# Carrying scores and weights between two orders of 50,000 edges: one-hot products for all 392 columns, or products for 248 and gathers for 144

## The chip, the cores and the metric

One Trainium2 chip, one of its cores. The metric is the device time of one execution in microseconds (us), and a kernel's time is the median of its runs. TensorE is called PE, VectorE DVE, ScalarE ACT, GpSimd POOL and SyncE SP, as in the profile.

## The reference, cut to what matters

The reference is four graph layers over 100,000 nodes (64 values each) and 50,000 edges. The change touches the second layer alone. There every edge has one score, the scores are turned into weights by a softmax over the edges that share a source node, and the weights scale the rows that are summed by target node:

```
e = leaky_relu(h[src] @ a_src + h[dst] @ a_dst, ALPHA)
seg_max = segment_max(e, src)
exp_e = exp(e - seg_max[src])
denom = segment_sum(exp_e, src)
attention = exp_e / denom[src]
h_prime = segment_sum(attention[:, None] * h[src], dst)
```

The edges are stored in the order of their targets. The softmax needs them in the order of their sources. So one value per edge is carried from the first order to the second before the softmax, and one value per edge is carried back after it.

## The kernel before, in words

The edges are padded to EP = 50176 = 128 x 392. A value per edge is one tile of 128 partitions and EF = 392 columns, and edge number i sits in partition i // 392, column i % 392. The prologue sorts the edges by source and leaves two lists in DRAM: EID says which edge of the first order stands at a place of the second, and RANK says at which place of the second order an edge of the first stands. Each is the inverse of the other.

The program is a row of blocks, each with its own instruction streams for the engines, and every block ends with a barrier of all engines. `weigh_edges` (L1591) runs five of them in a row: `pairs_block` makes the scores `e`; `permute_block` with tag `ps` carries them by RANK to `se`; `softmax_block` makes `sa`; `permute_block` with tag `pb` carries that by EID to `al`; a last block stores `al` to DRAM (L1606). Nothing else runs beside them. `mix_block` follows.

`permute_block` (L1450) works without any gather. SP loads the list of target places into `at` (L1467). DVE turns each place into its partition and its column, as floats (L1475 to L1480: `atf`, `near`, `part`, `col`). Then there is one step for each of the 392 columns c of the source. In it DVE makes two one-hot matrices: `lhs` (128 x 128), which has a one where the counter equals `part[:, c]` (L1485), and `rhs` (128 x 392), which has the value where the counter equals `col[:, c]` (L1486). PE multiplies them (L1495) and adds the product into one PSUM tile `sums` of 392 columns, so after 392 steps each value stands at its place. `lhs` and `rhs` have SL = 4 buffers each, and from the fifth step on DVE waits until PE has finished the step four before. At the end DVE copies `sums` to the output tile (L1489). ACT and POOL have nothing to do in the block.

Gathers and scatters elsewhere in the kernel are indirect DMAs that POOL issues, one for each column of 128 indices: L440 (one word per index, in the prologue, in batches of 8 with four semaphores in turn), L1141 (one word per index, into RANK), L802 and L1326 (rows of up to 66 words).

Of the kernel before, what the change touches and what calls it, by code (L numbers as in the profile page):

```python
# [8 lines left out]
I32 = mybir.dt.int32  # L9
# [3 lines left out]
P = 128  # L13
N, D = 100000, 64
E = 50000
# [3 lines left out]
EP = NCH * CH  # L19
EF = EP // P  # L20
# [137 lines left out]
def chunks_of(k, slots, total=NCH):  # L158

    return len(range(k, total, slots))  # L160
# [1286 lines left out]
NEAR = 12582912.0  # L1447


def permute_block(nc, T, C, tag, index, value, out):  # L1450

    with ExitStack() as ctx:
        m = Mem(nc, ctx, tag)
        SL = 4
        at = m.sb("at", [P, EF], I32)
        atf, near, part, col = (m.sb(x, [P, EF]) for x in "atf near part col".split())
        lhs = [m.sb(f"lhs{k}", [P, P]) for k in range(SL)]
        rhs = [m.sb(f"rhs{k}", [P, EF]) for k in range(SL)]  # L1460
        sums = m.ps("sums", [P, EF])
        s_at, s_ch, s_hot, s_mm = (m.sem(x) for x in "at ch hot mm".split())
        block = ctx.enter_context(nc.Block())

        @block.sync
        def _(sp):
            sp.dma_start(at[:, :], T[index][0:EP].rearrange("(p f) -> p f", f=EF)).then_inc(s_at, 16)  # L1467

        @block.vector
        def _(dve):  # L1470
            v = nc.vector
            ch = Chain(dve, s_ch, 0)
            ch.at(0)
            dve.wait_ge(s_at, 16)
            ch(v.tensor_copy(atf[:, :], at[:, :]))  # L1475

            ch(v.tensor_scalar(near[:, :], atf[:, :], 0.5 * (1 - EF), 1.0 / EF, ALU.add, ALU.mult))
            ch(v.tensor_scalar(near[:, :], near[:, :], NEAR, None, ALU.add))
            ch(v.tensor_scalar(part[:, :], near[:, :], -NEAR, None, ALU.add))
            ch(v.scalar_tensor_tensor(col[:, :], part[:, :], float(-EF), atf[:, :], ALU.mult, ALU.add))  # L1480
            for c in range(EF):
                k = c % SL
                if c >= SL:
                    dve.wait_ge(s_mm, c - SL + 1)
                v.tensor_scalar(lhs[k][:, :], C["count"][:, 0:P], part[:, c:c + 1], None, ALU.is_equal)  # L1485
                v.tensor_scalar(rhs[k][:, :], C["count"][:, :], col[:, c:c + 1], value[:, c:c + 1],  # L1486
                                ALU.is_equal, ALU.mult).then_inc(s_hot, 1)
            dve.wait_ge(s_mm, EF)
            ch(v.tensor_copy(out[:, :], sums[:, :]))  # L1489

        @block.tensor
        def _(pe):
            for c in range(EF):
                pe.wait_ge(s_hot, c + 1)
                nc.tensor.matmul(sums[:, :], lhs[c % SL][:, :], rhs[c % SL][:, :], start=(c == 0), stop=(c == EF - 1)  # L1495
                                 ).then_inc(s_mm, 1)
# [94 lines left out]
def weigh_edges(nc, T, C):  # L1591


    with ExitStack() as ctx:
        m = Mem(nc, ctx, "w")
        e, se, sa, al = (m.sb(x, [P, EF]) for x in "e se sa al".split())
        s_st = m.sem("st")
        pairs_block(nc, T, C, e)
        permute_block(nc, T, C, "ps", "RANK", e, se)
        softmax_block(nc, T, C, se, sa)  # L1600
        permute_block(nc, T, C, "pb", "EID", sa, al)
        with nc.Block() as block:

            @block.sync
            def _(sp):
                sp.dma_start(T["AL"].rearrange("(p f) -> p f", f=EF), al[:, :]).then_inc(s_st, 16)  # L1606
                sp.wait_ge(s_st, 16)
# [592 lines left out]
def program(nc, a, out):  # L2200
    T = {}

    def table(name, shape, dt=F32):
        T[name] = nc.dram_tensor(f"t_{name}", shape, dt, kind="Internal").ap()

    for name in ("SCAT", "POS", "PSRC", "KSRC", "KDST"):
        table(name, [EP], I32)
    for name in ("LAST", "KEEP", "ENDM", "ET"):
        table(name, [EP])
    table("XL", [N, XW])  # L2210
    T["EWP"] = nc.dram_tensor("t_EWP", [9, EP], BF16, kind="Internal").ap()
    table("EA", [18, EP])
    table("XSD", [EP, 2 * D])
    table("SSRC", [SORTED + 2])
    table("EID", [SORTED], I32)
    table("RANK", [SORTED], I32)
    table("AL", [EP])
    table("H1", [EP, P])
    table("HR", [EP, D])
    for name in ("D1", "D2", "D3", "HS", "AG", "X3", "HN3"):  # L2220
        table(name, [EP, D])
    for name in ("REL", "KS", "SL", "TL"):
        table(name, [EP])
    with ExitStack() as ctx:
        m = Mem(nc, ctx, "c")
        C = {name: m.sb(name, shape) for name, shape in (
            ("ident", [P, P]), ("att1r", [P, P]), ("att2r", [P, P]), ("att3r", [P, P]), ("att1b", [P, 8]),
            ("att2b", [P, 2]), ("att3b", [P, 4]), ("ones_row", [1, P]), ("wz1", [P, P]), ("we1", [1, P]),
            ("wl2", [P, P]), ("wr2", [P, P]), ("we2", [1, P]), ("wz3", [P, P]), ("we3", [P, P]), ("b1", [P, 1]),
            ("b2", [D, 1]),  # L2230
            ("b1row", [1, P]), ("brow", [1, P]), ("cstk", [P, D]), ("ones_sq", [P, P]),
            ("lng", [P, D]), ("lnb", [P, D]), ("lrg", [P, D]), ("lrb", [P, D]), ("gamma", [P, D]), ("beta", [P, D]),
            ("bias3", [P, D]), ("bias2", [P, D]), ("wca", [P, D]), ("wra", [P, D]), ("w1", [D, D]),
            ("a1", [D, 2]), ("wflat", [P, 2, 2, D]), ("w1t", [P, D]), ("wb", [P, P]), ("wft", [P, 2, P]),
            ("relp", [P, 2]), ("same", [P, EF]), ("count", [P, EF]), ("c3row", [1, D]), ("c3", [P, D]), ("k1", [P, D]), ("k0", [P, D]), ("bl3", [D, 1]), ("bsum", [P, P]))}
        for name in ("we1p", "we2p"):
            C[name] = m.sb(name, [9, P], BF16)
        C["at"] = m.sb("at", [P, 2, EF], I32)
        prologue_block(nc, a, T, C)
        gat_block(nc, a, T, C, "a", 8, P, False)  # L2240
        positions_block(nc, T)
        gat_block(nc, a, T, C, "b", 2, P, True)
        mlp_block(nc, T, C)
        logit_block(nc, T, C)
        weigh_edges(nc, T, C)
        mix_block(nc, T, C)
        relation_block(nc, T, C)
        gat_block(nc, a, T, C, "g", 4, D, False)
        batch_block(nc, T, C)
        finish_block(nc, a, T, out, C)  # L2250
# [24 lines left out]
```

## Time and profile before

| | before |
|---|---|
| median of 3 runs | 7306.34 us (7302.04 to 7308.86) |
| profiled execution, its own time | 7280.67 us |
| profiled execution, span of its instructions | 7278.9 us |
| mean granted PE clock over the span | 0.721 of full speed |
| block `ps`, from the issue of its load to the start of its last copy | 4004.55 to 4269.81 us |
| block `pb`, from its first matmul to the start of its last copy | 4309.0 to 4569.71 us |

The profile shows one execution. A row of a timeline gives the start, the duration, the engine, the line and the operation with the tiles it writes and reads; in square brackets stand the idle time of the engine before it and what ended that. A row of a table by stretch gives each engine's busy time, the number of instructions, and the clock that PE was granted (1.00 is 2.4 GHz, 0.50 is 1.2 GHz). Busy times of DVE and PE instructions overlap at their ends, so a rate is read from the distance of their starts, not from their durations.

### The profile page before, as it was taken

To read this page: it belongs to the slowest core of one execution; us is meant where nothing else is said; L and a number is where in the kernel's file an instruction comes from. 1 tells how busy PE (TensorE), PEld (TensorE's weight loads), DVE (VectorE), ACT (ScalarE), POOL (GpSimd) and SP (SyncE) were. 2 spreads that over 40 slices of the span, in tenths; PEclk is the share of its full clock that TensorE was granted. 3 is DMA by queue.
4 is the path that set the end of the run, shared out by engine and by line. 5 is a ranking of instruction groups with operands and counts; after the bars stand their busy time and mean duration, and the time that the engine had idled before them with its cause. 6 is when DMAs were issued, how large, how long until landed. Compare 5 with 4: busy or idle time off the path is not lost. (4 is left out here: it accounts for less than half of the span.)

```text
span 7278.9 us, 83566 instructions
## 1 busy us (share of the span) xinstructions
PE 3968.5 (55%) x13024; PEld 2369.0 (33%) x13024; DVE 5486.2 (75%) x16937; ACT 3171.6 (44%) x7568; POOL 4455.4 (61%) x4321
## 2 busy tenths in 40 slices
PE   0002666664665665997000989876886766773000
PEld 0000332322333334886000545672332433331000
DVE  4502898986777777887777999776887888886886
ACT  0001666663333333776444000124554666665555
POOL 2777777775777776775776000007664777774776
PEclk9999677776888887555555989558997676665555
DMA  6001555555333332212998000459884555554554
GB/s 190 4 1 34 99 98 98 100 98 81 87 85 84 86 85 61 49 47 57 121 118 102 2 5 1 136 150 129 155 152 108 116 113 115 113 115 110 169 167 136
DMA packets 905930, 687.04 MB, mean 94 GB/s; under 512 B 595425, under 2 KB 744702, under 8 KB 905180
## 3 DMA queue, kind: packets, MB, share of 16 engines
q1 hardware_dynamic: 517168, 403.39, 20.5%
q0 software_dynamic: 137984, 138.92, 18.9%
q10 hardware_dynamic: 250600, 143.02, 6.5%
q14 instruction: 147, 1.20, 0.1%
q8 instruction: 31, 0.51, 0.0%
HBM read 491.06 MB, written 227.24 MB: 99 GB/s over the span
## 5 line engine op out<-in xcount | busy, mean ns | idle before, releaser
L1793 POOL DMA_INDIRECT f_dg<-t_D,c_at x392 | 379.7, 969 | 1132.5 <-POOLq L179 943.3
L802 POOL DMA_INDIRECT b_xg<-t_H,c_at x784 | 828.4, 1057 | 286.0 <-issue 238.6
L802 POOL DMA_INDIRECT g_xg<-t_D,c_at x784 | 801.7, 1023 | 319.9 <-issue 237.7
L802 POOL DMA_INDIRECT a_xg<-t_XL,c_at x784 | 824.6, 1052 | 250.1 <-issue 238.7
L2181 POOL DMA_INDIRECT out<-n_yo,c_at x392 | 430.8, 1099 | 237.5 <-issue 116.0
L440 POOL DMA_INDIRECT t_XL<-su_pos,su_scatx x392 | 388.2, 990 | 244.7 <-DMA t_XL<-in_nodes 125.7
L1326 POOL DMA_INDIRECT l_d<-t_D,l_ix x392 | 399.3, 1019 | 174.8 <-issue 115.8
L1141 POOL DMA_INDIRECT t_RANK<-m_place,m_at x392 | 400.8, 1022 | 160.9 <-issue 115.7
L938 ACT ACTIVATE a_hn<-a_xg,a_sm 128x64 f32<-128x64 f32 x784 | 269.9, 429 | 399.0 <-DVE a_sm L675 398.0
L1375 ACT ACTIVATE l_hn<-l_xs,l_sm 128x64 f32<-128x64 f32 x784 | 265.0, 426 | 284.0 <-DVE l_sm L675 218.9
L2160 ACT ACTIVATE n_h<-n_x,n_sm 128x64 f32<-128x64 f32 (+1 forms) x800 | 269.4, 426 | 210.0 <-DVE n_sm L675 210.0
L1915 ACT ACTIVATE f_hn<-f_xs,f_bykind 128x64 f32<-128x64 f32 x784 | 265.1, 426 | 178.9 <-DVE f_bykind L1825 178.9
L1032 PE MATMUL b_bank<-c_ident,b_xg 128*128 128x128 f32 x392 | 93.6, 383 | 415.4 <-DMA b_xg<-t_H,c_at 415.4
L1060 PE MATMUL a_bank<-a_zt,c_att1r 128*128 128x512 f32 x196 | 196.4, 1105 | 221.2 <-DVE a_zt L850 221.2
L1416 PE MATMUL pr_prow<-c_ident,pr_col 128*1 128x128 f32 x2 | 0.6, 395 | 567.0 <-DVE pr_col L1434 567.0
L1035 PE MATMUL a_bank<-c_ident,a_hn 128*128 128x128 f32 x392 | 108.4, 432 | 369.1 <-ACT a_hn L938 369.0
L938 ACT ACTIVATE g_hn<-g_xg,g_sm 128x64 f32<-128x64 f32 x784 | 269.6, 427 | 76.4 <-DVE g_sm L675 76.2
L1060 PE MATMUL g_bank<-g_zt,c_att3r 128*128 128x512 f32 x196 | 159.5, 907 | 258.2 <-DVE g_zt L850 258.2
L958 ACT ACTIVATE b_hT<-b_bank 128x512 f32<-128x512 f32 x98 | 58.5, 597 | 521.1 <-PE b_bank L1035 521.1
L1253 ACT ACTIVATE m_xn<-m_pa,m_sm 128x64 f32<-128x64 f32 x784 | 242.4, 414 | 90.5 <-DVE m_sm L675 89.1
L1704 ACT ACTIVATE e_ng<-e_pw 128x256 f32<-128x256 f32 x98 | 37.5, 383 | 535.2 <-PE e_pw L1695 535.2
L1495 PE MATMUL pb_sums<-pb_rhs,pb_lhs 128*128 128x392 f32 x784 | 260.6, 496 | 11.3 <-DVE pb_rhs L1486 11.3
(451 smaller groups left out, 13667.4 us busy)
## 6 DMA issues: line engine op xcount, KB each, us to landing
a_ends<-t_LAST SPq DMA_DIRECT2D x98, 256.0 KB
t_XSD<-a_xg SPq DMA_DIRECT2D x98, 256.0 KB
t_H<-a_oE ACTq DMA_DIRECT2D x98, 256.0 KB
b_ends<-t_LAST SPq DMA_DIRECT2D x98, 256.0 KB
l_xb<-t_XSD SPq DMA_DIRECT2D x49, 512.0 KB
f_rl<-t_REL SPq DMA_DIRECT2D x49, 512.0 KB
g_xb<-t_XSD SPq DMA_DIRECT2D x98, 256.0 KB
g_ends<-t_LAST SPq DMA_DIRECT2D x98, 256.0 KB
```

The costliest lines, as they stand in the source:

```text
L440: nc.gpsimd.indirect_dma_start(lp, bass.IndirectOffsetOnAxis(ap=scatx[:, f:f + 1], axis=0), pos[:, f:f + 1].bitcast(F32), None, bounds_che ...
L802: nc.gpsimd.indirect_dma_start(xg[k][:, j, i, :], None, table, bass.IndirectOffsetOnAxis(ap=C["at"][:, i, n * J + j:n * J + j + 1], axis=0 ...
L938: last = f(hn[k][:, g // 2, g % 2, :], xg[k][:, g // 2, g % 2, 0:D], ACT.Relu, bias=sm[:, 5, g:g + 1], scale=sm[:, 4, g:g + 1])
L1060: mm(bS[:, :], att[:, :], zt[k][:, :], start=True, stop=True).then_inc(S["s"], 1)
L1141: nc.gpsimd.indirect_dma_start(rank, bass.IndirectOffsetOnAxis(ap=at[k][:, j:j + 1], axis=0), place[k][:, j:j + 1], None).then_inc(s_rank[ ...
L1326: nc.gpsimd.indirect_dma_start(d1[k][:, 0, j, :], None, T["D1"], bass.IndirectOffsetOnAxis(ap=ix[k][:, j:j + 1], axis=0)).then_inc(s_g[k], 16)
L1375: last = nc.scalar.activation(hn[k][:, g % 2, g // 2, :], xs[k][:, g // 2, g % 2, :], ACT.Relu, bias=sm[:, 5, g:g + 1], scale=sm[:, 4, g:g ...
L1495: nc.tensor.matmul(sums[:, :], lhs[c % SL][:, :], rhs[c % SL][:, :], start=(c == 0), stop=(c == EF - 1)).then_inc(s_mm, 1)
L1793: nc.gpsimd.indirect_dma_start(dg[k][:, u, j, :], None, T["D2"], bass.IndirectOffsetOnAxis(ap=C["at"][:, 0, (2 * n + u) * J + j:(2 * n + u ...
L1915: last = f(hn[k][:, g // J, g % J, c, :], xs[k][:, g // J, g % J, :], ACT.Relu, bias=by_kind[:, c, 1, g:g + 1], scale=by_kind[:, c, 0, g:g ...
L2160: last = f(h[k][0:np_, g, :], x[k][0:np_, g, :], ACT.Relu, bias=sm[0:np_, 5, g:g + 1], scale=sm[0:np_, 4, g:g + 1])
L2181: nc.gpsimd.indirect_dma_start(out, bass.IndirectOffsetOnAxis(ap=C["at"][:, 0, j:j + 1], axis=0), yo[:, j, :], None, bounds_check=N - 1, o ...
```

## The change: what it does

`permute_block` takes a second list, the inverse of the first, and splits the 392 result columns in two. Columns 0 to 247 are made by products as before: `rhs`, `sums` and the last copy are 248 wide, and there are still 392 steps of `lhs`, `rhs` and product. Columns 248 to 391 are fetched: ACT stores the value tile to a table in DRAM (new tables Vps and Vpb), SP loads the part of the inverse list that belongs to these columns into `of`, DVE clears those columns of the output, and when all three are done POOL issues 144 indirect DMAs. Each fetches 128 single words of the table into one column. They go in 18 batches of 8 with four semaphores in turn, so that a batch waits for the one four before it. POOL ends its part when all have landed. Both calls of `permute_block` get it.

```diff
--- before.py
+++ after.py
@@ -1447,7 +1447,11 @@
 NEAR = 12582912.0
 
 
-def permute_block(nc, T, C, tag, index, value, out):
+BY_GATHER = 144
+BY_PRODUCT = EF - BY_GATHER
+
+
+def permute_block(nc, T, C, tag, index, inverse, value, out):
 
 
 
@@ -1457,20 +1461,45 @@
         at = m.sb("at", [P, EF], I32)
         atf, near, part, col = (m.sb(x, [P, EF]) for x in "atf near part col".split())
         lhs = [m.sb(f"lhs{k}", [P, P]) for k in range(SL)]
-        rhs = [m.sb(f"rhs{k}", [P, EF]) for k in range(SL)]
-        sums = m.ps("sums", [P, EF])
-        s_at, s_ch, s_hot, s_mm = (m.sem(x) for x in "at ch hot mm".split())
+        rhs = [m.sb(f"rhs{k}", [P, BY_PRODUCT]) for k in range(SL)]
+        of = m.sb("of", [P, BY_GATHER], I32)
+        sums = m.ps("sums", [P, BY_PRODUCT])
+        s_at, s_ch, s_hot, s_mm, s_of, s_value, s_clear = (m.sem(x) for x in "at ch hot mm of value clear".split())
+        s_g = m.sems("g", 4)
         block = ctx.enter_context(nc.Block())
+        full = lambda t: t.rearrange("(p f) -> p f", f=EF)
 
         @block.sync
         def _(sp):
-            sp.dma_start(at[:, :], T[index][0:EP].rearrange("(p f) -> p f", f=EF)).then_inc(s_at, 16)
+            sp.dma_start(at[:, :], full(T[index][0:EP])).then_inc(s_at, 16)
+            sp.dma_start(of[:, :], full(T[inverse][0:EP])[:, BY_PRODUCT:EF]).then_inc(s_of, 16)
+
+        @block.scalar
+        def _(act):
+            act.dma_start(full(T["V" + tag]), value[:, :]).then_inc(s_value, 16)
+
+        @block.gpsimd
+        def _(pool):
+            pool.wait_ge(s_of, 16)
+            pool.wait_ge(s_value, 16)
+            pool.wait_ge(s_clear, 1)
+            for b in range(BY_GATHER // 8):
+                k = b % 4
+                if b >= 4:
+                    pool.wait_ge(s_g[k], 16 * 8 * (b // 4))
+                for f in range(8 * b, 8 * b + 8):
+                    nc.gpsimd.indirect_dma_start(out[:, BY_PRODUCT + f:BY_PRODUCT + f + 1], None, T["V" + tag].unsqueeze(1),
+                                                 bass.IndirectOffsetOnAxis(ap=of[:, f:f + 1], axis=0),
+                                                 bounds_check=E - 1, oob_is_err=False).then_inc(s_g[k], 16)
+            for k in range(4):
+                pool.wait_ge(s_g[k], 16 * 8 * chunks_of(k, 4, BY_GATHER // 8))
 
         @block.vector
         def _(dve):
             v = nc.vector
             ch = Chain(dve, s_ch, 0)
             ch.at(0)
+            v.memset(out[:, BY_PRODUCT:EF], 0.0).then_inc(s_clear, 1)
             dve.wait_ge(s_at, 16)
             ch(v.tensor_copy(atf[:, :], at[:, :]))
 
@@ -1483,10 +1512,10 @@
                 if c >= SL:
                     dve.wait_ge(s_mm, c - SL + 1)
                 v.tensor_scalar(lhs[k][:, :], C["count"][:, 0:P], part[:, c:c + 1], None, ALU.is_equal)
-                v.tensor_scalar(rhs[k][:, :], C["count"][:, :], col[:, c:c + 1], value[:, c:c + 1],
+                v.tensor_scalar(rhs[k][:, :], C["count"][:, 0:BY_PRODUCT], col[:, c:c + 1], value[:, c:c + 1],
                                 ALU.is_equal, ALU.mult).then_inc(s_hot, 1)
             dve.wait_ge(s_mm, EF)
-            ch(v.tensor_copy(out[:, :], sums[:, :]))
+            ch(v.tensor_copy(out[:, 0:BY_PRODUCT], sums[:, :]))
 
         @block.tensor
         def _(pe):
@@ -1596,9 +1625,9 @@
         e, se, sa, al = (m.sb(x, [P, EF]) for x in "e se sa al".split())
         s_st = m.sem("st")
         pairs_block(nc, T, C, e)
-        permute_block(nc, T, C, "ps", "RANK", e, se)
+        permute_block(nc, T, C, "ps", "RANK", "EID", e, se)
         softmax_block(nc, T, C, se, sa)
-        permute_block(nc, T, C, "pb", "EID", sa, al)
+        permute_block(nc, T, C, "pb", "EID", "RANK", sa, al)
         with nc.Block() as block:
 
             @block.sync
@@ -2219,7 +2248,7 @@
     table("HR", [EP, D])
     for name in ("D1", "D2", "D3", "HS", "AG", "X3", "HN3"):
         table(name, [EP, D])
-    for name in ("REL", "KS", "SL", "TL"):
+    for name in ("REL", "KS", "SL", "TL", "Vps", "Vpb"):
         table(name, [EP])
     with ExitStack() as ctx:
         m = Mem(nc, ctx, "c")
```

## Rows read from the trace of the kernel before

**Rows 1.** Busy time of each engine over the whole span (page, part 1).

```profile
PE 3968.5 (55%) x13024; PEld 2369.0 (33%) x13024; DVE 5486.2 (75%) x16937; ACT 3171.6 (44%) x7568; POOL 4455.4 (61%) x4321
```

**Rows 2.** Busy us by stretch inside ps and pb; PE, PEld, DVE, ACT, POOL, clock, DMA.

```profile
4050.00:4250.00 200.00, 200.00 (x609) 115.47 (x608) 200.00 (x608) 0.00 (x0) 0.00 (x0) 1.00 0.00 1
4350.00:4550.00 200.00, 200.00 (x609) 115.48 (x608) 200.00 (x609) 0.00 (x0) 0.00 (x0) 1.00 0.00 1
```

**Rows 3.** Timeline, start of block ps: load, first four steps, first wait.

```profile
4004.55 0.33 SPq L1467 DMA_DIRECT2D ps_at<-t_RANK  x1
4006.68 0.36 DVE L1475 CAST ps_atf<-ps_at 128x392 f32<-128x392 int32 x1 [2.84 <-DMA ps_at<-t_RANK]
...
4009.48 0.28 DVE L1485 TENSOR_SCALAR ps_lhs<-c_count,ps_part 128x128 f32<-128x128 f32 x1
...
4009.68 0.48 DVE L1486 TENSOR_SCALAR ps_rhs<-c_count,ps_col,w_e 128x392 f32<-128x392 f32 x1
4010.07 0.28 DVE L1485 TENSOR_SCALAR ps_lhs<-c_count,ps_part 128x128 f32<-128x128 f32 x1
...
4012.64 0.29 DVE L1485 TENSOR_SCALAR ps_lhs<-c_count,ps_part 128x128 f32<-128x128 f32 x1 [0.62 <-PE ps_sums L1495]
```

**Rows 4.** Timeline, end of block ps: the last step's first instruction, the copy.

```profile
4267.18 0.29 DVE L1485 TENSOR_SCALAR ps_lhs<-c_count,ps_part 128x128 f32<-128x128 f32 x1
...
4269.81 0.57 DVE L1489 COPY w_se<-ps_sums 128x392 f32<-128x392 f32 x1 [1.95 <-PE ps_sums L1495]
```

**Rows 5.** Lines L667 and L378, TENSOR_SCALAR of DVE: count, ns min/median/max, starts.

```profile
L667 DVE TENSOR_SCALAR a_sm<-a_sm x98: 171/194/427, 667.9 to 1723.0; 128x8 int32<-128x8 int32 x98
...
L378 DVE TENSOR_SCALAR su_sign<-su_bits x16: 426/428/599, 110.2 to 254.6; 128x512 f32<-128x512 int32 x16
```

**Rows 6.** The store of the last block and the next block's first load.

```profile
4571.17 0.34 SPq L1606 DMA_DIRECT2D t_AL<-w_al  x1
4573.86 0.33 SPq L1642 DMA_DIRECT2D e_hs<-t_HS  x1
```

**Rows 7.** Busy us by stretch, three stages with POOL issuing indirect DMAs (L440, L802, L1141).

```profile
500.00:600.00 100.00, 0.00 (x0) 0.00 (x0) 0.00 (x0) 0.00 (x0) 75.99 (x79) 1.00 0.02 1
1000.00:1200.00 200.00, 135.74 (x351) 61.40 (x352) 179.31 (x551) 123.69 (x291) 155.19 (x148) 0.70 0.54 98
3000.00:3200.00 200.00, 182.71 (x846) 161.27 (x846) 176.67 (x919) 149.35 (x425) 154.27 (x151) 0.50 0.19 48
```

**Rows 8.** Timeline: two instances of L667, each inside one indirect DMA.

```profile
3606.12 0.94 POOL L1326 DMA_INDIRECT l_d<-t_D,l_ix  x1 [0.30 <-issue]
3606.79 0.27 DVE L667 TENSOR_SCALAR l_sm<-l_sm 128x16 int32<-128x16 int32 x1
...
677.13 0.94 POOL L802 DMA_INDIRECT a_xg<-t_XL,c_at  x1 [0.30 <-issue]
...
677.85 0.22 DVE L667 TENSOR_SCALAR a_sm<-a_sm 128x8 int32<-128x8 int32 x1
```

**Rows 9.** Timeline: two large TENSOR_SCALAR back to back beside an indirect DMA.

```profile
203.25 1.16 POOL L440 DMA_INDIRECT t_XL<-su_pos,su_scatx  x1 [0.30 <-issue]
203.60 0.43 DVE L376 TENSOR_SCALAR su_bits<-su_gray 128x512 int32<-128x512 int32 x1
204.06 0.60 DVE L378 TENSOR_SCALAR su_sign<-su_bits 128x512 f32<-128x512 int32 x1
...
204.71 0.97 POOL L440 DMA_INDIRECT t_XL<-su_pos,su_scatx  x1 [0.30 <-issue]
```

**Rows 10.** Timeline: POOL and a long DVE instruction that read SBUF together.

```profile
3602.52 1.23 DVE L1342 TENSOR_TENSOR l_xs<-l_d,l_xb 128x1024 f32<-128x1024 f32 x1 [2.96 <-DMA l_d<-t_D,l_ix]
3602.57 1.99 POOL L1326 DMA_INDIRECT l_d<-t_D,l_ix  x1 [0.30 <-issue]
```

**Rows 11.** Busy us by stretch: stages where PE is less busy than in ps.

```profile
800.00:1000.00 200.00, 134.62 (x348) 59.92 (x348) 180.25 (x546) 127.16 (x301) 155.19 (x148) 0.72 0.54 100
5100.00:5300.00 200.00, 177.89 (x534) 73.20 (x533) 174.89 (x540) 110.63 (x304) 130.54 (x135) 0.93 0.88 155
```

## The prediction

> **What bounds the kernel now.** The page's busy times come first [rows 1]. They name no bound for this change: DVE's 75% is a mean over stages, and `permute_block` runs alone between barriers. So I read its two blocks by stretch [rows 2]. PE and DVE are both busy for all of each 200 us, POOL and ACT do nothing, and PE has its full clock, 2.4 GHz. 609 product instructions, two for a step, make 304.5 steps in 200 us: 0.657 us a step. Which of the two engines sets this shows at the start of the block. In its first steps, with free buffers, DVE starts an `lhs` every 0.59 us (4009.48, 4010.07), 0.20 us of it for `lhs` and 0.39 for `rhs`; after four buffers it waits for PE [rows 3]. PE is the bound, and DVE is only 10% faster. From the first `lhs`, one step of 0.59 us before the 4009.48 [rows 3], to the last at 4267.18 the steps take 258.3 us; then 2.6 us pass to the copy [rows 4]. Seen from the issue of the load at 4004.55, the copy starts after 265.3 us.
>
> **The products.** A product of 248 columns instead of 392 takes 0.657 x 248/392 = 0.416 us of PE. DVE's `lhs` stays at 0.20. For `rhs` I need the price of a column. A one-input instruction took 0.428 us for 512 columns [rows 5] and 0.36 for 392 [rows 3], which is 0.55 ns each. If the whole distance between the 0.20 us slot of 128 columns and the 0.39 us slot of 392 were width, it would be 0.72 ns, the upper end. I take 0.55, which compares instructions without a pointer in both widths: 144 x 0.55 = 0.08 us. DVE's step becomes 0.51 us. So the bound moves from PE (0.416) to DVE (0.51), and only part of PE's 37% arrives: 392 x 0.51 = 200 us. With 0.72 ns it would be 0.486 and 191 us.
>
> **The load, the store, the clear, the copy.** The new store and the second load are issued beside the old load, by ACT and behind it on SP's queue; nothing waits behind them. DVE first used the old load 2.1 us after its issue [rows 3]; for three transfers together I add 1 us, between 0 and 2. The clear of 144 columns goes into DVE's 2.8 us wait for the load [rows 3]; without that cover it is under 0.6 us, the copy of 392 columns [rows 4]. The last copy is narrower (under 0.2 us gained). PE no longer lags by four buffers, so of the 2.6 us before the copy about 1 goes. These cancel.
>
> **The gathers.** POOL needs the store to have landed. A store of the same size and the barrier after it fit into 2.7 us [rows 6], so I start the gathers 3 us after the block's first issue. 144 follow. POOL alone issued 79 in 100 us, 1.27 us each; with DVE 90% busy beside it 148 in 200 us, 1.35 each, and 151 in another stage, 1.32 [rows 7]. With 2 us for the last to land (the load's 2.1) the end is 5 + 144 x 1.35 = 199 us. The traffic is small, 128 words an instruction; the stage at 151 in 200 us moved single words too [rows 7]. So the gathers lie beside the products as long as one costs less than (231 - 5)/144 = 1.57 us, 231 being the end of the products below.
>
> **What they do to each other.** In no stretch of the kernel do wide one-input DVE instructions run without a break beside POOL, so this cost is bounded. A TENSOR_SCALAR that takes 0.171 us took up to 0.427 beside a gather [rows 5]. Two of these late ones end in the same hundredth as the POOL instruction around them (3606.79 + 0.27 = 3606.12 + 0.94; 677.85 + 0.22 = 677.13 + 0.94) [rows 8]. So POOL seems to hold something late in each indirect DMA that DVE needs, for up to 0.256 us. A wide one lost 0.171 us (0.599 against 0.428) [rows 5, 9]. POOL also waits: beside a long two-input instruction its 0.94 became 1.99 [rows 10]. With DVE at work without a gap I take 0.171 us lost per gather, since that row has DVE's shape of instruction: 144 x 0.171 = 25 us on DVE, which now bounds. The ends are 0 and 0.256 + 0.171 = 0.427 (both losses in each gather), 61 us. No gain is possible from a wait. For POOL I allow the 0.19 us that its instruction lost beside that pair (1.16 against 0.97 for the next at that line) [rows 9]: 1.35 + 0.19 = 1.54, ending at 227, still hidden, but barely.
>
> The Trainium skill, "SBUF — State Buffer", section "Who interferes with whom", says more than the row: DVE in a two-port mode and GpSimd exclude each other for the whole of an instruction, whoever starts first. The row shows a hold of at most 0.256 us of 0.94, so here it agrees only in kind. What the whole rule would cost is the third rival.
>
> **The sum.** The step phase becomes 200 + 25 = 225 us instead of 258.3; the copy starts 4.3 + 225 + 1.6 = 231 us after the block's first issue. That is 33 us less, twice 33 = 66 us. On the profiled execution, 7280.7 us (1.8 more than its span), this gives 7215; the median of the runs is 25.6 higher, and against it I predict 7306 - 66 = 7240 us. This case's own range: with no loss and 191 us, 67 less per block, 7172; with the loss at 0.427, 261 us, nothing gained, 7306.
>
> **The rivals.**
> *The gathers end the block but late by less than the gain.* At 1.7 us a gather the end is 5 + 245 = 250 us instead of 265.3: 15 less per block, 7276. For it speaks that my 1.54 is near 1.57. Against it: 1.35 in stages with DVE 90% busy.
> *The gathers starve (slower).* POOL finds DVE in its way at every issue. The point from which it decides is (265.3 - 5)/144 = 1.81 us a gather. At 2.0 the block ends at 293, 28 more, 7362; at the 1.99 + 0.30 of [rows 10] at 335, 7445. For it speaks that DVE never pauses here. Against it: that row's DVE instruction lasted 1.23 us, while these last 0.48 at most.
> *Whole exclusion.* (The rule of the Trainium skill named above gives this one.) If each gather held DVE off for all of its 0.94 us: 144 x 0.94 = 135, a phase of 335 us, 77 more per block, 7460. Against it: in [rows 9] the first TENSOR_SCALAR ran its normal 0.43 us inside the gather.
> *The clock.* PE would be at work 0.416 of 0.57 us, 73%, instead of all the time. Stages with PE 89% busy had a granted clock of 0.93, with 67% one of 0.72 [rows 11]. At 1.2 GHz a step is 0.83 us, the phase 326, 68 more per block, 7442. Against it: those stages do not feed PE in a steady beat, and a slower PE would be fully busy again, which in [rows 2] goes with the full clock.
> *Nothing is left.* The loss per gather is near its upper bound and takes the whole gain: 7306.
>
> **How the numbers follow.** A measurement can tell about 0.2%, 15 us. Forecast 0.60; gathers late but gaining 0.12; nothing left 0.08; starving 0.10; whole exclusion 0.06; clock 0.04. Faster by over 0.2%: 0.60 + 0.12 = 0.72. Same: 0.08. Slower: 0.10 + 0.06 + 0.04 = 0.20. The range reaches from 7185, near the lower bound of the forecast, over the late gathers and the nothing-left case to 7320, where it leaves out most of the three slower ones, 0.17.
>
> **What would show it.** Starts of `lhs` about 0.51 us apart where no gather is in flight and 0.57 on average; PE at 7 to 8 tenths of its time with clock 1.00; DVE's instructions lengthened inside gathers, in sum near 25 us a block; 144 gathers 1.35 to 1.54 us apart, the last landed before DVE's copy; the copy at about 231 us. The forecast is wrong if the copy or the block's end waits for POOL, if gathers are over 1.57 us apart, if the clock falls inside the block, or if a TENSOR_SCALAR lasts a whole gather.

## The result, and the profile after

The changed kernel took 7208.85 us (median of 4 runs, 7205.54 to 7228.42). The kernel before, beside it on the same chip, took 7307.60 (7302.04 to 7313.52). The ratio is 0.987, with a 95% interval from 0.9851 to 0.989: 98.7 us faster, where 66 were forecast. On a second kind of chip, met later in the study, the same kernel is slower than the one before (below).

The profiled execution of the change took 7206.94 us, its span 7205.2. The busy line of its page answers to [rows 1]. DVE did 100 us less and POOL 305 us more:

```profile
PE 3879.4 (54%) x13024; PEld 2314.5 (32%) x13024; DVE 5386.3 (75%) x16939; ACT 3173.0 (44%) x7568; POOL 4760.7 (66%) x4609
```

The table by stretch of the change (busy us of PE, PEld, DVE, ACT, POOL, then the granted PE clock) has block `ps` beside the gathers, `ps` after the last gather, and `pb` beside the gathers. It answers to [rows 2]:

```profile
4040.00:4220.00 180.00, 180.00 (x663) 98.32 (x662) 180.00 (x663) 0.00 (x0) 139.78 (x133) 1.00 0.02 1
4228.00:4244.00 16.00, 16.00 (x64) 9.23 (x62) 16.00 (x64) 0.00 (x0) 0.00 (x0) 1.00 0.00 0
4292.00:4470.00 178.00, 178.00 (x677) 100.32 (x675) 178.00 (x677) 0.00 (x0) 136.90 (x135) 1.00 0.02 1
```

Half the number of products is the number of steps: 0.543 us a step beside gathers in `ps` and 0.526 in `pb`, against 0.657 before. PE kept its full clock of 2.4 GHz. PE and DVE both show as fully busy because their records overlap, so the rows alone don't say which engine waits. The timeline of the change at the start of `ps` does more:

```profile
4026.93 0.37 ACTq L1479 DMA_DIRECT2D t_Vps<-w_e  x1
4026.93 0.33 SPq L1474 DMA_DIRECT2D ps_at<-t_RANK  x1
...
4029.99 0.36 DVE L1504 CAST ps_atf<-ps_at 128x392 f32<-128x392 int32 x1 [2.78 <-DMA ps_at<-t_RANK]
...
4031.48 1.01 POOL L1491 DMA_INDIRECT w_se<-t_Vps,ps_of  x1 [45.36 <-DMA ps_of<-t_EID]
```

DVE has the list 3.06 us after the first issue (2.13 before, [rows 3]), and the first gather starts 4.55 us after it. Near the end of the gathers:

```profile
4217.15 0.27 DVE L1514 TENSOR_SCALAR ps_lhs<-c_count,ps_part 128x128 f32<-128x128 f32 x1
...
4217.67 0.27 DVE L1514 TENSOR_SCALAR ps_lhs<-c_count,ps_part 128x128 f32<-128x128 f32 x1
...
4217.70 1.11 POOL L1491 DMA_INDIRECT w_se<-t_Vps,ps_of  x1 [0.30 <-issue]
...
4218.38 0.52 DVE L1515 TENSOR_SCALAR ps_rhs<-c_count,ps_col,w_e 128x248 f32<-128x248 f32 x1
4218.82 0.27 DVE L1514 TENSOR_SCALAR ps_lhs<-c_count,ps_part 128x128 f32<-128x128 f32 x1
...
4225.87 1.12 POOL L1491 DMA_INDIRECT w_se<-t_Vps,ps_of  x1 [0.30 <-issue]
...
4245.86 0.42 DVE L1518 COPY w_se<-ps_sums 128x248 f32<-128x248 f32 x1 [0.78 <-PE ps_sums L1524]
```

The `lhs` start 0.52 us apart without an idle time in brackets, so DVE doesn't wait for PE here (in all 784 steps it did so three times, 0.6 us in sum). The `rhs` that runs into the last part of the gather took 0.52 us instead of 0.40, and that gather 1.11 instead of 1.00. The whole of `ps` has this rhythm: five steps go with two gathers. An `rhs` is lengthened in 72 of the 144 gathers, in nearly every second one, and it starts 0.68 us into the gather (median). In the other 72 the `rhs` at the gather's end starts 0.95 us into it and takes its normal 0.40. In `pb` the rhythm is shifted by 0.04 us: 71 `rhs` that start 0.72 us into a gather took 0.47 us. The last gather ends 19 us before the copy, so nothing waits for POOL.

The profiled executions of before and after differ by only 74 us, since that of before was 27 us below the median of 7307.60: `ps` began at 4004.55 before and at 4026.93 after, a difference from stages that the change leaves alone. So I compare the blocks, each from its first issue to the start of its copy. This table is worked out from the two traces. The loss per gather is (step beside gathers minus step after them) x steps beside gathers / 144.

```
us                    before ps  before pb   change ps  change pb
first issue to copy      265.3      266.3       218.9      213.3
mean step                0.661      0.662       0.543      0.528
gather to gather                                1.359      1.321
last gather ends at                             200.1      194.8
step beside / after                      .5454/.5149  .5295/.5148
loss per gather                                 0.076      0.036
```

The blocks give 46.3 + 53.1 = 99.4 us, within 1 us of the measured 98.7.

### The profile page after: what moved, and what is told of

It is laid out like the page before. It is cut to its first block and busy times, and to the rows that moved or that the text cites. A ratio compares the mean times of both kernels' runs of the same rounds, so it can differ in the third digit from the quotient of the medians.

```text
span 7205.2 us, 84156 instructions
## 1 busy us (share of the span) xinstructions
PE 3879.4 (54%) x13024; PEld 2314.5 (32%) x13024; DVE 5386.3 (75%) x16939; ACT 3173.0 (44%) x7568; POOL 4760.7 (66%) x4609
## 5 line engine op out<-in xcount | busy, mean ns | idle before, releaser
L802 POOL DMA_INDIRECT b_xg<-t_H,c_at x784 | 833.2, 1063 | 284.0 <-issue 238.4
L802 POOL DMA_INDIRECT g_xg<-t_D,c_at x784 | 803.4, 1025 | 320.1 <-issue 238.2
L802 POOL DMA_INDIRECT a_xg<-t_XL,c_at x784 | 830.6, 1059 | 250.3 <-issue 238.8
L440 POOL DMA_INDIRECT t_XL<-su_pos,su_scatx x392 | 389.8, 994 | 245.6 <-DMA t_XL<-in_nodes 126.4
L1141 POOL DMA_INDIRECT t_RANK<-m_place,m_at x392 | 397.9, 1015 | 163.2 <-issue 116.4
```

The lines of the kernel that those rows point to most:

```text
L440: nc.gpsimd.indirect_dma_start(lp, bass.IndirectOffsetOnAxis(ap=scatx[:, f:f + 1], axis=0), pos[:, f:f + 1].bitcast(F32), None, bounds_che ...
L802: nc.gpsimd.indirect_dma_start(xg[k][:, j, i, :], None, table, bass.IndirectOffsetOnAxis(ap=C["at"][:, i, n * J + j:n * J + j + 1], axis=0 ...
L1141: nc.gpsimd.indirect_dma_start(rank, bass.IndirectOffsetOnAxis(ap=at[k][:, j:j + 1], axis=0), place[k][:, j:j + 1], None).then_inc(s_rank[ ...
```

## The experiments

Four kernels ran first, on a chip where the kernel before takes 7306.35 us (19 runs). My theory: PE bounded the step before, DVE bounds it now, and the gathers cost only what they take from DVE. The rivals: the gain has another cause than the width of both engines, or the gathers cost as such.

**No gathers.** The store, the second load and the clear stay; 144 columns of the result are left out.

```diff
-            for b in range(BY_GATHER // 8):
...
-            for k in range(4):
-                pool.wait_ge(s_g[k], 16 * 8 * chunks_of(k, 4, BY_GATHER // 8))
```

> The changed kernel without its 144 gathers per block (columns 248 to 391 stay zero; store, second load and clear remain). Theory (DVE bounds the steps at its free-running 0.516 us, and each gather takes a little from it): every step 0.516 us, the copy starts about 209 us after the block's first issue in both blocks, instead of 219.0 in ps and 213.2 in pb, so about 14 us less than the changed kernel, near 7194 us. Rival (the gathers cost DVE nothing, the two blocks differ for another reason): blocks stay at 219 and 213, time near 7208.

**Gathers beside full products.** Products of 392 columns as before, and the same 144 gathers into a tile that nobody reads.

```diff
+        rhs = [m.sb(f"rhs{k}", [P, EF]) for k in range(SL)]
+        spare = m.sb("spare", [P, EF])
...
+                    nc.gpsimd.indirect_dma_start(spare[:, BY_PRODUCT + f:BY_PRODUCT + f + 1], None, T["V" + tag].unsqueeze(1),
...
+                v.tensor_scalar(rhs[k][:, :], C["count"][:, :], col[:, c:c + 1], value[:, c:c + 1],
```

> All 392 columns by products as before, and the 144 gathers beside them into a tile that nothing reads. Theory (the loss per gather is under 0.1 us, and DVE has 0.06 us to spare in each 0.657 us step that PE bounds): DVE's step is 0.59 plus 0.48 gathers times 0.075 = 0.63 us, still under 0.657; the copy starts 265 to 268 us after the first issue, time as before. Rival (each gather takes 0.171 us of DVE, as the prediction had it): DVE's step becomes 0.675, blocks 7 to 9 us longer, time 14 to 18 us longer than before, and PE waits for DVE all through.

**PE narrow alone.** DVE makes `rhs` 392 wide, PE multiplies 248 columns of it; no gathers.

```diff
+                v.tensor_scalar(rhs[k][:, :], C["count"][:, :], col[:, c:c + 1], value[:, c:c + 1],
...
+                nc.tensor.matmul(sums[:, :], lhs[c % SL][:, :], rhs[c % SL][:, 0:BY_PRODUCT], start=(c == 0), stop=(c == EF - 1)
```

> DVE still makes rhs 392 wide, PE multiplies only 248 of its columns, no gathers (columns 248 to 391 stay zero). Theory (DVE is the bound as soon as PE is under 0.59): step 0.593 us, the copy starts about 239 us after the first issue, 27 less per block than before, time near 7254. Rival (the gain of the change is all PE's): step as in the changed kernel, 0.52 us, blocks near 209, time near 7194.

**DVE narrow alone.** DVE writes 248 columns of a 392-wide `rhs` whose rest was cleared once, PE multiplies all 392; no gathers.

```diff
+            for t in rhs:
+                v.memset(t[:, BY_PRODUCT:EF], 0.0)
...
+                v.tensor_scalar(rhs[k][:, 0:BY_PRODUCT], C["count"][:, 0:BY_PRODUCT], col[:, c:c + 1], value[:, c:c + 1],
```

> DVE makes rhs 248 wide inside a 392 wide tile whose other columns are zero, PE multiplies all 392, no gathers (columns 248 to 391 stay zero). Theory (PE bounds before): step stays 0.657 us, blocks 265 to 268 us, time as before, 7307. Rival (DVE bounds before, PE's full share of busy time is only its model): step falls to 0.52 to 0.6 us, time 7200 to 7260.

Measured, with the block from first issue to copy in `ps` and `pb`, and the mean step in `ps`:

```
                      us        ratio (95%)             ps     pb    step
no gathers         7191.78  0.9844 (0.9827 to 0.986)  209.6  209.2  .518
beside full        7303.86  0.9998 (0.9988 to 1.0007) 266.5  266.6  .661
PE narrow alone    7248.00  0.9924 (0.9908 to 0.9941) 237.8  238.5  .591
DVE narrow alone   7304.50  0.9998 (0.9988 to 1.0007) 267.2  267.5  .662
```

The same stretch of the table by stretch in these four, in this order:

```profile
4050.00:4200.00 150.00, 150.00 (x584) 86.67 (x584) 150.00 (x584) 0.00 (x0) 0.00 (x0) 1.00 0.00 1
```

```profile
4050.00:4200.00 150.00, 150.00 (x457) 86.55 (x456) 150.00 (x457) 0.00 (x0) 115.36 (x114) 1.00 0.02 1
```

```profile
4050.00:4200.00 150.00, 150.00 (x510) 75.57 (x509) 150.00 (x511) 0.00 (x0) 0.00 (x0) 1.00 0.00 1
```

```profile
4050.00:4200.00 150.00, 150.00 (x457) 86.57 (x456) 138.01 (x457) 0.00 (x0) 0.00 (x0) 1.00 0.00 1
```

These four settle the first part. A narrower `rhs` for DVE alone changes nothing: the same 457 products in 150 us, with DVE at 138 of them. A narrower product alone brings the step to 0.59 us, DVE's free step of [rows 3]: PE was the bound, and DVE's own step was only 10% shorter than PE's. Both together bring 0.518. The 114 gathers in the second fence cost nothing as long as PE bounds. Beside the DVE-bound step all 288 cost 7208.85 - 7191.78 = 17 us together (the kernel before took 7307.60 and 7306.35 beside them); 13 us of it are in the two blocks.

**Another split of the columns, one-hot tiles with a step of two words, and a shorter DVE step.** Two other counts of gathers were to give the price of one gather from a slope. The strided tiles, which DVE writes and PE reads with a step of two words, were to slow DVE's writes, and with that to take away the loss. The last one was meant to beat the change: one two-input instruction makes `lhs` for four steps.

```diff
-BY_GATHER = 144
+BY_GATHER = 96
```

> The change with 96 columns gathered and 296 by products. Theory (a column costs DVE 0.54 ns: 0.593 - 0.516 us over 144; a gather 0.076 us in ps, 0.036 in pb): free step 0.516 + 48 x 0.00054 = 0.542 us, 212 us of steps, plus 7 and 3; the copy starts about 226 and 222 us after the first issue, 16 us more than the change in sum, near 7224 us. PE (0.657 x 296/392 = 0.496) is still under DVE. Rival (the losses come from POOL being late, not from each gather): no loss remains, blocks near 219, and the time stays within 5 us of the change, 7208 to 7213.

With 168 in that line:

> 168 columns gathered, 224 by products. Theory: the products end at about 392 x 0.503 + 13 + 7 = 216 (ps) and 210 us (pb) after the first issue, but POOL ends only at 4.5 + 168 x 1.359 + 2 = 235 and 4.9 + 168 x 1.321 + 2 = 229, so the next block waits for POOL: its start is 16 us later per block than with 144, time near 7240. Rival (gathers become faster with fewer DVE columns, or DVE ends the block still): time 7195 to 7208.

```diff
+        lhs = [m.sb(f"lhs{k}", [P, 2 * P]) for k in range(SL)]
+        rhs = [m.sb(f"rhs{k}", [P, 2 * BY_PRODUCT]) for k in range(SL)]
...
+                v.tensor_scalar(rhs[k][:, 0:2 * BY_PRODUCT:2], C["count"][:, 0:BY_PRODUCT], col[:, c:c + 1], value[:, c:c + 1],
```

> lhs and rhs written and read with a step of two words, so that DVE should write one word a cycle and not two; otherwise the change (248 by products, 144 gathered). Read for the loss per gather: the step while gathers run against the step after them. Theory (the loss comes from the form of DVE instruction that writes two words a cycle and needs what POOL holds): the step grows to 0.7 us or more, blocks of 275 us or more, and the steps beside gathers are within 0.01 us of the steps after them, loss per gather under 0.02 us. Rival (any DVE instruction loses): loss per gather stays 0.036 to 0.076 us.

```diff
+BY_GATHER = 136
...
+                if c % KL == 0:
+                    if c >= 2 * KL:
+                        dve.wait_ge(s_mm, c - KL)
+                    v.tensor_tensor(lhs[c // KL % 2][:, :, :], C["count"][:, 0:P].unsqueeze(1).to_broadcast([P, KL, P]),
+                                    part[:, c:c + KL].unsqueeze(2).to_broadcast([P, KL, P]), ALU.is_equal)
```

> A version meant to be faster: lhs is made for four steps by one two-input instruction of 512 columns (is_equal of the counter and four columns of part), and 136 columns are gathered, 256 by products. Theory (DVE bounds, and what it saves comes off the block): lhs costs 0.59/4 = 0.15 us a step instead of 0.20, rhs 0.32, step 0.47; with a loss of 0.076 per gather the copy starts at 5 + 184 + 10 + 2 = 201 us in ps and 196 in pb, about 35 us less than the change in sum, 7174. The gathers would end at 4.5 + 136 x 1.36 + 2 = 191. Rival (the wide two-input instruction and POOL keep each other waiting, 0.5 us each time): gathers 1.6 to 1.8 us apart, ending at 220 to 250 us, no gain or slower than the change.

These four came to a chip of another kind. There the kernel before takes 8575.02 us (7 runs, 8547.91 to 8599.4), and all four are slower than it. The expectations, made for the first kind, missed by far.

```
                    us        ratio (95%)             ps     pb   last gather   loss per
                                                                 ends at (ps)   gather
96 gathers       8687.38  1.0139 (1.0106 to 1.0172)  321.1  327.4   131.5      0.98
168 gathers      8843.91  1.031 (1.0269 to 1.0351)   406.6  404.3   223.1      1.09
strided          8792.16  1.0265 (1.0222 to 1.0308)  379.0  379.6   192.2      1.07
lhs by four      8754.65  1.0206 (1.0171 to 1.024)   355.5  352.4   182.7      1.10
```

A gather came every 1.30 to 1.33 us, near the first kind's, and DVE lost about 1 us to each. From some 8 to 17 us after the last gather on, the steps ran as fast as DVE can make them: 0.47 us with the `lhs` by four, as expected. In the strided kernel they were no slower than the change's (table by stretch, 196 DVE instructions in 50 us, 0.51 us a step):

```profile
4990.00:5040.00 50.00, 50.00 (x195) 30.29 (x195) 50.00 (x196) 0.00 (x0) 0.00 (x0) 1.00 0.00 1
```

So a step of two words did not slow DVE's writes, and that run did not test what it was meant to test.

**The change again, and the counter in PSUM.** Both ran on yet another chip, of the first kind (before: 7281.88, 13 runs). In the second kernel DVE reads the counter out of PSUM, for `lhs` and for `rhs`.

> The changed kernel itself, unedited, once more, because the last four kernels ran on a second chip of the same kind on which the kernel before takes 8575 us instead of 7306, and on which DVE hardly made a step while gathers ran. Theory (on that chip DVE is held off for nearly the whole of each gather): on the second chip the gathers end 193 us after the block's first issue with about 55 steps made, the other 337 follow at 0.516 us, so the copy starts about 367 us after it instead of 266; the change is about 200 us slower than before, ratio 1.023. On the first chip again: 219 and 213 us, ratio 0.987. Rival (the loss belonged to the four edits, not to the chip): ratio near 0.987 on either chip.

```diff
+            ch(v.tensor_copy(count[:, :], C["count"][:, 0:BY_PRODUCT]))
...
+                v.tensor_scalar(lhs[k][:, :], count[:, 0:P], part[:, c:c + 1], None, ALU.is_equal)
+                v.tensor_scalar(rhs[k][:, :], count[:, :], col[:, c:c + 1], value[:, c:c + 1],
```

> The change with the counter that both one-hot instructions read moved from SBUF to PSUM, so that DVE takes its wide input from PSUM and not from SBUF and writes one word a cycle; everything else is the same. From the copies out of PSUM (392 columns 567 ns, 248 columns 417 ns) a column costs 1.04 ns: step 0.71 to 0.75 us when free. Theory (the loss beside gathers is that the instruction with two words a cycle out of SBUF needs what POOL holds): no loss, steps beside gathers as long as those after them to 0.01 us on either chip, gathers 1.25 to 1.30 us apart, the copy starts 283 to 300 us after the first issue; 35 to 70 us slower than before on the first chip, and over 100 us faster than the unedited change on the second. Rival (DVE is held off by something all its instructions need): loss per gather stays 0.04 to 0.08 us on the first chip and near 1.07 us on the second, where the blocks would last over 420 us.

The change again took 7175.4, ratio 0.9851 (0.9828 to 0.9875), with `ps` at 215.6 us and `pb` at 218.8 and losses of 0.055 and 0.074 per gather. The order of the blocks is reversed against the first profile, so their difference is no property of a block. It goes with the rhythm: here it is `pb` whose 72 lengthened `rhs` took 0.52 us, and `ps` whose 69 took 0.47.

With the counter in PSUM: 7309.23, ratio 1.0038 (1.0028 to 1.0047), blocks of 281.4 and 281.7 us. It is 27 us slower than the kernel before, where 35 to 70 were expected. The table by stretch of that kernel, beside the gathers and after them:

```profile
4020.00:4180.00 160.00, 156.41 (x457) 67.90 (x456) 160.00 (x458) 0.00 (x0) 122.54 (x124) 1.00 0.02 1
4200.00:4280.00 80.00, 78.21 (x229) 33.93 (x229) 80.00 (x229) 0.00 (x0) 0.00 (x0) 1.00 0.00 1
```

458 DVE instructions in 160 us and 229 in 80 are the same 0.70 us a step: the loss per gather is zero. The gathers don't suffer either. The tile's rows give count, ns minimum, median and maximum, and first and last start; first this kernel, then the change:

```profile
L1492 POOL DMA_INDIRECT w_se<-t_Vps,ps_of x144: 992/997/1009, 4007.7 to 4193.7; - x144
...
L1517 DVE TENSOR_SCALAR ps_rhs<-ps_count,ps_col,w_e x392: 512/515/530, 4009.0 to 4283.4; 128x248 f32<-128x248 f32 x196
```

```profile
L1491 POOL DMA_INDIRECT w_se<-t_Vps,ps_of x144: 993/1008/1120, 4031.5 to 4225.9; - x144
...
L1515 DVE TENSOR_SCALAR ps_rhs<-c_count,ps_col,w_e x392: 392/398/617, 4032.4 to 4244.7; 128x248 f32<-128x248 f32 x196
```

With the wide input in PSUM an `rhs` takes 0.515 us instead of 0.398, and neither engine is ever lengthened much: maxima of 530 and 1009 ns, where the change has 617 and 1120. So the loss on the first kind of chip belongs to the fast form, with its wide input in SBUF: 0.50 ns a column, from the steps of 0.591 and 0.518 us that are 144 columns apart. The source and the rate changed together in this run, so which of the two decides is not separated. What the loss cost in a block (9 us on average) is less than the slow form costs (65 us). The Trainium skill, "SBUF — State Buffer", section "Who interferes with whom", has DVE's two-port modes and GpSimd exclude each other. The rows agree in that the loss is gone when the wide input leaves SBUF. They do not agree with an exclusion over the whole instruction: 0.036 to 0.076 us were lost to a gather of 1.0, on average.

**The change on the second kind, and half of the `lhs` by ACT.** They ran on another chip of the second kind (before: 8452.91, 11 runs). In the second kernel ACT makes the `lhs` of the odd steps, as 1 - (count - part)² cut off at zero, so DVE's step gets shorter; 128 gathers.

> The changed kernel once more on the chip of the version before it in this call. Theory: where the kernel before takes near 7300 us, ratio 0.985 to 0.987, copies 213 to 219 us after the first issue. Where it takes near 8575 us, ratio 1.023, copies near 367 us. Rival (the change is faster on every chip, and the four kernels that were slower there were so by their edits): ratio near 0.987 there too.

```diff
+                    last = f(far[g % 2][:, i, :], C["count"][:, 0:P], ACT.Square, bias=part[:, c:c + 1], scale=-1.0)
...
+                f(odd[g % 3][:, :, :], far[g % 2][:, :, :], ACT.Relu, bias=1.0, scale=-1.0).then_inc(s_odd, 1)
...
+                if c % 2 == 0:
+                    v.tensor_scalar(lhs[c // 2 % SL][:, :], C["count"][:, 0:P], part[:, c:c + 1], None, ALU.is_equal)
```

> A version meant to beat both: ACT, idle in the block, makes the lhs of every second step (Square of part minus counter, then Relu of 1 minus that, which is one where they are equal and zero elsewhere), DVE makes the others and all rhs; 128 columns are gathered, 264 made by products. Theory (DVE bounds and what is taken from it comes off the block until PE or the gathers bound): DVE's step 0.32 + 0.10 = 0.42 us plus 0.03 for the gathers, PE's 0.657 x 264/392 = 0.443; the copy starts 180 to 188 us after the first issue instead of 213 to 219, the gathers end at about 181; 60 to 75 us faster than the change, ratio to before 0.975 to 0.980. Rival (ACT is too slow or waits in turn with DVE and PE): step over 0.5 us, no better than the change. On the second kind of chip (before 8575 us) DVE is held off during the gathers, the blocks are near 330 us, slower than before.

The change took 8676.02 here, ratio 1.0256 (1.0222 to 1.029): 223 us slower than the kernel before. Its blocks are 376.8 and 376.7 us long. Ratio 1.023 and 367 us were expected for this kind. The table by stretch, beside the gathers and long after them:

```profile
4690.00:4870.00 180.00, 52.26 (x107) 23.18 (x105) 31.51 (x103) 0.00 (x0) 138.03 (x138) 0.53 0.02 1
...
4990.00:5040.00 50.00, 50.00 (x196) 28.88 (x196) 50.00 (x195) 0.00 (x0) 0.00 (x0) 1.00 0.00 1
```

After the gathers a step takes 0.51 us, as on the first kind. Beside them DVE is busy 31.5 of 180 us, and PE, with little to do, falls to a clock of 0.53. Where DVE stands shows in the groups from 4684 to 4870 (x instructions | busy us, mean ns | idle us just before them and what ended it):

```profile
L1515 DVE TENSOR_SCALAR ps_rhs<-c_count,ps_col,w_e 128x248 f32<-128x248 f32 x61 | 26.1, 427 | 0.0
L1514 DVE TENSOR_SCALAR ps_lhs<-c_count,ps_part 128x128 f32<-128x128 f32 x61 | 18.4, 301 | 147.2 <-DMA l_d<-t_D,l_ix 100.7 <-issue 34.2 <-PE ps_sums L1524 12.0
```

and in the timeline of that kernel:

```profile
4783.68 0.29 DVE L1514 TENSOR_SCALAR ps_lhs<-c_count,ps_part 128x128 f32<-128x128 f32 x1 [4.96 <-issue]
4783.89 0.40 DVE L1515 TENSOR_SCALAR ps_rhs<-c_count,ps_col,w_e 128x248 f32<-128x248 f32 x1
...
4789.28 0.34 DVE L1514 TENSOR_SCALAR ps_lhs<-c_count,ps_part 128x128 f32<-128x128 f32 x1 [4.99 <-DMA l_d<-t_D,l_ix]
4789.37 1.00 POOL L1491 DMA_INDIRECT w_se<-t_Vps,ps_of  x1 [0.30 <-issue]
4789.55 0.40 DVE L1515 TENSOR_SCALAR ps_rhs<-c_count,ps_col,w_e 128x248 f32<-128x248 f32 x1
```

An `lhs` begins 5.6 us after the one before it, four gathers later. All 147 us of idle time stand before `lhs`, which waits for the semaphore `s_mm` that PE increments after each product. None stands before `rhs`, which has no wait of its own and takes its normal 0.40 us, also inside a gather. The DMA named as releaser belongs to a tile of an earlier stage and is no cause. An exclusion over each instruction would leave DVE 0.30 us of every 1.30; 144 of these are 43 us, room for 84 steps of 0.51. There were 61, and it would have put off `rhs` too. So what is held here is the start behind a semaphore wait, for up to 5 us, not the access of one instruction. The other kernels on this kind agree, worked out from their traces in `ps`: with the `lhs` by four the wait for the next increment stands before each `rhs`, and so do 157 us of idle time, with 0.0 before `lhs`; with ACT's share (below) it stands before `lhs` and `rhs` in turn, and they have 76 and 75 us.

The traces also record the increments of `s_mm`. In the first profile and the repeat on the first kind all of them, in both blocks, are recorded within 0.1 us after the end of a product, mostly 0.01. On the second kind, beside the gathers of `ps`, 38% are, and half of them are recorded over 0.9 us after one. Of the 31 starts of `lhs` there that were held for over 1 us, 24 come within 0.05 us after a recorded increment. PE itself starts 0.05 us after an `rhs` ends, on both kinds. So by these records DVE starts at once when the increment is there, and the increment comes late although PE has finished. The trace lacks some increments (45 of 61 are in it), so the count is rough, and why they are late is open. Nor does the hold go with a single gather: the distance between two `lhs` grew from 0.5 to 5.6 us in the first 50 us of gathers, and the last held starts lie 13 us (`ps`) and 14 us (`pb`) behind the end of the last gather.

The kernel's other stages show the same. The groups of the stage that makes the edge logits, in the repeat of the change on the first kind of chip and then on the second (L661 and L664 wait for a semaphore, L672 does not):

```profile
L661 DVE TENSOR_TENSOR l_sm<-l_bn 128x16 f32<-128x16 f32 x46 | 8.6, 186 | 1.6
...
L664 DVE TENSOR_TENSOR l_sm<-l_sm 128x16 f32<-128x16 f32 x46 | 8.1, 175 | 1.6
...
L672 DVE SCALAR_TENSOR_TENSOR l_sm<-l_sm 128x16 f32<-128x16 f32 x46 | 7.7, 168 | 0.0
```

```profile
L661 DVE TENSOR_TENSOR l_sm<-l_bn 128x16 f32<-128x16 f32 x44 | 8.2, 186 | 61.6 <-DMA t_PSRC<-c_at 50.5 <-issue 7.5 <-DVE l_bn L649 2.7
...
L664 DVE TENSOR_TENSOR l_sm<-l_sm 128x16 f32<-128x16 f32 x44 | 7.8, 177 | 25.5 <-DMA t_PSRC<-c_at 12.1 <-DVE l_sm L663 9.0 <-issue 3.5
...
L672 DVE SCALAR_TENSOR_TENSOR l_sm<-l_sm 128x16 f32<-128x16 f32 x44 | 7.5, 170 | 0.0
```

These three instructions last as long on either kind; only the idle time before the waiting ones differs. In two blocks POOL issues nothing: `mix_block`, from its first DVE instruction to the end of its last, took 332.2 us in the repeat on the first kind and 331.5 on the second, and the softmax block 26.6 on either (the same measure). Outside the two permuting blocks the repeat took 1185 us more on the second kind, and the kernel before 1171 us more (8452.91 against 7281.88). That the same late starts make up all of it is likely and not shown, since no trace of the kernel before was taken there. The kernel before has no indirect DMAs in the two permuting blocks; the change brings the hold into them.

With ACT's share the kernel took 8599.04, ratio 1.0168 (1.0135 to 1.02), with blocks of 335.9 and 337.7 us, near the 330 that were expected for this kind. Its stretch after the gathers:

```profile
4900.00:4950.00 50.00, 50.00 (x227) 42.69 (x226) 50.00 (x170) 31.14 (x85) 0.00 (x0) 1.00 0.00 1
```

227 products in 50 us are 0.44 us a step instead of 0.51. It beats the change by 77 us on this chip and still loses to the kernel before. It and the `lhs` by four were only run on the second kind. Whether they beat the change on the first kind is open, and so is the counter in PSUM on the second.

## Why the prediction was right, and where it was not

**The bound.** "PE is the bound, and DVE is only 10% faster" is shown by the two runs that narrow one engine alone: 0.59 us with PE narrow, no change with DVE narrow.

**The products.** DVE's free step was put at 0.51 from 0.55 ns a column (its two rows give 0.57, which makes the same 0.08 us) and measured 0.515. The other price of a column (0.72 ns, 0.486 us) is out. PE's 0.416 fits under it with room, since DVE waited for PE in three of 784 steps.

**The small parts.** I let load, store, clear and copy cancel. The load came 0.9 us later, as estimated (1), the clear ran in its cover, and from the last `lhs` (4244.50) to the copy 1.4 us passed, where 1.6 were put.

**The gathers.** They start after 4.55 and 4.91 us (put at 3) and come every 1.32 to 1.36 us (put at 1.35, at most 1.54). They end after 195 to 200 us (put at 199 to 227), ahead of the copy. On the first kind of chip the three rivals with late, starving or wholly excluded gathers are out, and so is the clock: PE was granted 2.4 GHz beside the gathers in both blocks.

**The step that was mis-sized** is "I take 0.171 us lost per gather, since that row has DVE's shape of instruction". Measured were 0.076 and 0.036 in the first profile, 0.055 and 0.074 in the repeat. In the first profile that is 11 and 5 us a block instead of 25. With it the step phase is 212 and 207 us, not 225. The copy was put at 231 us, which leaves out the 1 us for the load; with it, 232 is the 33 us less that were counted. It stands at 219 and 213 us: 13 + 19 us, of the 33 by which the forecast fell short. The rest is that the kernel before ran 1 us longer in `pb` than in `ps`, and rounding. The row was a maximum, one of sixteen. Its size was near what an `rhs` in `ps` lost when a gather's late part met it: 11 us over 72 are 0.15 us. What failed is "per gather": only 72 of the 144 gathers in `ps` did that, and the 71 in `pb` cost 0.07 us each. The bounds of 0 and 0.427 held.

**What the prediction did not see** is that the sign depends on the chip. It rests on rows of one chip, and for that kind its range holds (the repeat's 7175 us lie below it, but beside 7282 for the kernel before; 106 us less than 7306 are 7200). On the second kind the steps took 370 us, beyond the 335 of whole exclusion, the rival nearest to it, and by late starts behind semaphore waits instead. No row of the kernel before could have shown it on the first kind of chip.

## What to carry to other kernels

Work out both engines' free steps before narrowing a step that two engines share: a 37% narrower product made the block 17 to 20% shorter, because the other engine took over as the bound, at 0.51 us a step. Take a loss between engines that is read from single rows as a bound and not as a mean: the row tells what one meeting costs, and how often the two meet depends on the rhythm of both. Before moving work to indirect DMAs beside a dense stream of short, semaphore-driven DVE instructions, time it on several chips: the same change gave -1.3% and -1.5% in two comparisons on one kind and +2.6% on another kind.

## What the runs showed of the hardware that was not expected

- There are two kinds of chips here, by their behaviour: the kernel before took 7282 and 7306 us on two (7308 in the runs of the result), 8453 and 8575 us on two others. Each chip was met in one group of runs only, so a lasting property of a chip and a state that passes are not told apart. On the second kind DVE instructions behind a semaphore wait start some 5 us late while POOL issues indirect DMAs, and up to 17 us after the last one; PE starts 0.05 us after its `rhs`. It is not a longer instruction, and PE has long finished: most of these waits end at a recorded increment of the semaphore that comes late. Why it comes late was not found.
- Beside gathers, DVE's fast form out of SBUF lost 0.04 to 0.08 us to each gather of 1.0 us on average: 0.15 or 0.07 us in nearly every second one. With the wide input in PSUM DVE lost 0.000, at 0.70 instead of 0.51 us a step.
- A tile written with a step of two words (fp32) kept the fast rate: 0.51 us a step for 128 and 248 columns.
- 144 indirect DMAs of 128 single words each cost POOL 1.00 us and 0.30 us of issue, 1.30 us each at the least; beside the densest DVE work of this kernel it was 1.36.
